# Cluster sums in bf16 parts for half of each third unit, and folded before the selection matmul

## The reference

```python
idx = jnp.argmax(sim, axis=1)                    # sim: normalised x against normalised centroids
onehot = jax.nn.one_hot(idx, N, dtype=x.dtype)
sum_x = jnp.einsum('bhwn,bchw->bnc', onehot, x)  # the cluster sums
count = jnp.sum(onehot, axis=(1, 2))
centroids_local = sum_x / jnp.maximum(count, 1.0)[..., None]
gathered = centroids_local[jnp.arange(B)[:, None, None], idx]
delta = jnp.transpose(gathered, (0, 3, 1, 2)) - x
alpha = jnp.exp(-jnp.mean(delta * delta, axis=1, keepdims=True))
y = x + alpha * delta
out = relu(jnp.einsum('oc,bchw->bohw', W, y) + b)
```

## Time and profile before

| | us |
|---|---|
| median of three runs | 411.43 (411.01 to 411.76) |
| the profiled execution | 411.51 |
| its span in the trace | 409.7 |
| outside the span | 1.8 |
| TensorE busy | 404.5 (99%) |
| VectorE busy | 334.1 (82%) |
| GpSimd busy | 262.9 (64%) |
| ScalarE busy | 257.6 (63%) |

### The profile page before, as it was taken

How to read it: one execution, slowest core, us unless ns; L and a number is a source line. 1 busy time by engine, 2 the same in 40 slices (tenths; PEclk the granted TensorE clock), 3 DMA queues, 4 the chain that set the end, 5 groups by cost and what they waited for, 6 DMA issues and landing times.

```text
span 409.7 us, 5780 instructions
## 1 busy us (share of the span) xinstructions
PE 404.5 (99%) x2090; PEld 289.8 (71%) x2095; DVE 334.1 (82%) x408; ACT 257.6 (63%) x355; POOL 262.9 (64%) x117
## 2 busy tenths in 40 slices
PE   9999999999999999999999999999999999999997
PEld 6755476775777677775867757776777758777886
DVE  3349999788989879899798889898798996898730
ACT  6666774677565594665764676655846657576641
POOL 2003874975699486993789846995869937434420
PEclk9999999999999999999999999999999999999999
DMA  8993574969598596957879485984956240222213
GB/s 268 373 239 55 107 241 93 300 222 218 175 268 201 138 267 148 274 157 191 240 205 269 143 205 172 257 229 133 263 147 215 105 141 2 102 102 104 102 71 136
DMA packets 77917, 74.51 MB, mean 182 GB/s; under 512 B 13722, under 2 KB 52890, under 8 KB 77890
## 3 DMA queue, kind: packets, MB, share of 16 engines
q1 hardware_dynamic: 77890, 74.15, 65.1%
HBM read 46.22 MB, written 25.17 MB: 174 GB/s over the span
## 4 chain that ended last, share of the span: by engine, by line
PE 96%; POOL 1%; ACT 1%; issue 0%; DVE 0%; ACTq 0%; POOLq 0%
PE main L983 21%; PE main L984 21%; PE main L985 21%; PE fa L878 11%; PE sump L923 8%; PE gat L961 5%; PE fa L887 1%; PE al L967 1%; PE main L1043 1%; PE al L1021 1%; PE main L996 1%; PE al L972 1%; POOL o L379 1%; POOL o L382 1%; PE gat L996 0%; PE main L1014 0%
## 5 line engine op out<-in xcount | busy, mean ns | idle before, releaser
L983 PE MATMUL main<-yh,wh 128*128 128x512 f32 (+1 forms) x376 | 152.8, 406 | 0.0
L984 PE MATMUL main<-yl,wh 128*128 128x512 f32 (+1 forms) x376 | 146.3, 389 | 0.0
L985 PE MATMUL main<-yh,wl 128*128 128x512 f32 (+1 forms) x376 | 146.2, 389 | 0.0
L357 POOL TENSOR_TENSOR z<-z,x 128x1024 f32<-128x1024 f32 x41 | 98.5, 2421 | 67.8 <-DVE z L504 67.8
L364 POOL TENSOR_TENSOR yl<-z,yh 128x1024 fp32r<-128x1024 f32 x43 | 103.7, 2432 | 8.2 <-ACT yh L669 8.1
L677 ACT ACTIVATE o<-main,bcol 128x512 f32<-128x512 f32 x96 | 65.2, 681 | 58.5 <-PE main L985 58.2
L983 PEld LDWEIGHTS main<-yh,wh 128*128 128x128 f32 x376 | 70.6, 188 | 21.4 <-issue 4.6
L985 PEld LDWEIGHTS main<-yh,wl 128*128 128x128 f32 x376 | 70.6, 188 | 15.0
L984 PEld LDWEIGHTS main<-yl,wh 128*128 128x128 f32 x376 | 70.7, 188 | 13.9
L371 POOL TENSOR_TENSOR xr<-xt 128x2048 f32<-128x2048 f32 x11 | 51.5, 4682 | 18.2 <-DVE xt L408 18.2
L471 DVE TENSOR_TENSOR z<-gat,x 128x1024 f32<-128x1024 f32 x46 | 56.0, 1218 | 5.4 <-PE gat L961 5.1
(11 more groups left out here) (137 smaller groups left out, 398.2 us busy)
## 6 DMA issues: line engine op xcount, KB each, us to landing
out<-o SPq DMA_DIRECT2D x23, 1024.0 KB, 7.2
x<-x SPq DMA_DIRECT2D x21, 1024.0 KB, 6.8
xs<-x SPq DMA_DIRECT2D x76, 256.0 KB, 5.5
x<-x SPq DMA_DIRECT2D x12, 256.0 KB, 4.5
o<-w SPq DMA_DIRECT2D x1, 1024.0 KB, 8.6
out<-o SPq DMA_DIRECT2D x3, 256.0 KB, 2.0
out<-o SPq DMA_DIRECT2D x2, 128.0 KB, 1.7
oht<-oh SPq DMA_TRANSPOSE x7, 3.7
```

The lines of the kernel that those rows point to most:

```text
L357: pool.tensor_tensor(z, z, X[g // PARTS % 2][:, pair(h), span(g)], ALU.add).then_inc(y_pool, 1)
L983: t_.matmul(tile, WH[:, k, rows], YH[g % 2][:, k, cols], start=(k == 0), stop=False)
L984: t_.matmul(tile, WH[:, k, rows], YL[g % 2][:, k, cols], start=False, stop=False)
L985: last = t_.matmul(tile, WL[:, k, rows], YH[g % 2][:, k, cols], start=False, stop=(k == KC - 1))
```

## The change

1. `split(g)` now returns a number of tiles: four for places 0 and 1 as before, two (HALF) for place 2 of images 2 to 7. So the first two tiles of six units (8, 11, 14, 17, 20, 23) are summed in three bf16 parts too. GpSimd makes their first rest into a new buffer `XRH`, VectorE their second rest.
2. The third unit's other two tiles are summed first, in float32, and its split half last. A pair of matmuls now takes neighbouring tiles.
3. From image 1 on the two halves of `sumP` are added before the high part is made: ScalarE moves the upper half to `upper_sum` (`move_sums`), VectorE adds (`fold_clusters`), ScalarE makes the high part (`copy_sums`), VectorE the low part into partitions 64 to 103 of the same tile, and `add_halves` is one matmul. It stands behind nine of the twelve matmuls of the convolution's second block.
4. VectorE's transposes stand three in the first step, one in the second and two in the third. `add_squares` is cut into `add_pair` (twice) and `add_pairs`, with `low_clusters` between the two.

```diff
 def split(g):
-    return g > 2 * PARTS and g % PARTS < SPLIT
+    return (TILES if g % PARTS < SPLIT else HALF) if g > 2 * PARTS else 0
...
 def sum_order(b):
-    return (0, 1, 2) if b == 0 else (1, 2, 0) if b == 1 else (2, 0, 1)
+    order = (0, 1, 2) if b == 0 else (1, 2, 0)
+    if b < 2:
+        return [(u, range(HALF)) for u in order]
+    return [(2, range(1, HALF)), (0, range(HALF)), (1, range(HALF)), (2, range(1))]
...
+        XRH = sb("xrh", [P, HALF, C], F32)
...
             def first_rest(g):
                 pool.wait_ge(tr_done, by_vector(g))
-                xt = XT[:, g % PARTS, :, :]
-                pool.tensor_tensor(XR[:, g % PARTS, :, :].rearrange("p t c -> p (t c)"),
+                xt = XT[:, g % PARTS, 0:split(g), :]
+                pool.tensor_tensor(rests(g % PARTS).rearrange("p t c -> p (t c)"),
...
             def second_rest(g):
                 dve.wait_ge(rest1_done, splits(g))
-                xr = XR[:, g % PARTS, :, :]
+                xr = rests(g % PARTS)
...
+            def fold_clusters(b):
+                dve.wait_ge(moved_done, b)
+                own = sumP[column_tiles[0], :]
+                v_.tensor_tensor(own, upper_sum[0:N, :], own, ALU.add).then_inc(folded_done, 1)
+
             def low_clusters(b):
                 dve.wait_ge(sumsH_done, b + 1)
...
+                    dve.wait_ge(cop_done, b)
+                    v_.tensor_tensor(sumsH[column_tiles[1], :], sumP[column_tiles[0], :],
+                                     sumsH[column_tiles[0], :].bitcast(F32), ALU.subtract).then_inc(sumsL_done, 1)
...
                 if beside and p < 2:
-                    transpose_half(g + 4, 0)
+                    transpose_half(g + 4, p)
+                if beside and p == 2:
+                    fold_clusters(b + 1)
+                    counts(b + 1)
+                add_pair(g, 0)
                 if beside and p == 2:
                     low_clusters(b + 1)
-                    counts(b + 1)
-                add_squares(g)
+                add_pair(g, 1)
+                add_pairs(g)
                 if beside and p == 0:
                     transpose_half(g + 4, 1)
                 fold(g)
+                if beside and p == 0:
+                    transpose_half(g + 5, 0)
...
                     first_best(b + 1)
-                    transpose_half(g + 4, 1)
...
-                if g + 3 < UNITS and split(g + 3):
+                if p < SPLIT and g + 3 < UNITS and split(g + 3):
                     second_rest(g + 3)
+                if p == 1 and g + 4 < UNITS and split(g + 4):
+                    second_rest(g + 4)
...
             def move_upper(g):
                 act.wait_ge(s_done, folded(g))
+                act.wait_ge(folded_done, min((g + 1) // PARTS, BATCH - 1))
...
+            def move_sums(b):
                 act.wait_ge(c_done, PARTS * (b + 1))
-                wait(act, cop_done, b)
-                a_.activation(sumsH[:, :], sumP[:, :], ACT.Copy).then_inc(sumsH_done, 1)
+                wait(act, fold_done, folded(PARTS * b - 2))
+                a_.activation(upper_sum[0:N, :], sumP[column_tiles[1], :], ACT.Copy).then_inc(moved_done, 1)
...
                 square(g, 0)
                 if beside and p == 2:
+                    move_sums(b + 1)
+                    count_onehot(b + 1)
+                    square(g, 1)
                     copy_sums(b + 1)
-                    count_onehot(b + 1)
                     high_half(g - 1, 0)
-                    square(g, 1)
                     relu(g - 2, 0)
...
                     convolve(g - LAG, 0)
+                    convolve(g - LAG, 1, ks=range(KC - 1))
                     add_halves(b + 1)
+                    convolve(g - LAG, 1, ks=range(KC - 1, KC))
```

More of the change, by code:

```diff
@@ L69, in split @@
 def split(g):
-    return g > 2 * PARTS and g % PARTS < SPLIT
+    return (TILES if g % PARTS < SPLIT else HALF) if g > 2 * PARTS else 0
 def splits(g):
-    return sum(split(i) for i in range(g + 1))
+    return sum(split(i) > 0 for i in range(g + 1))
 def sum_order(b):
-    return (0, 1, 2) if b == 0 else (1, 2, 0) if b == 1 else (2, 0, 1)
+    order = (0, 1, 2) if b == 0 else (1, 2, 0)
+    if b < 2:
+        return [(u, range(HALF)) for u in order]
+    return [(2, range(1, HALF)), (0, range(HALF)), (1, range(HALF)), (2, range(1))]
 def by_vector(g):
@@ L569, in _ @@
             y_half(0, 1)
+            fold_clusters(1)
+            scale(1, 0)
             low_clusters(1)
-            scale(1, 0)
             scale(1, 1)
@@ L780, in _ @@
             high_half(0, 0)
-            copy_sums(1)
+            move_sums(1)
             exp(1)
             high_half(0, 1)
+            copy_sums(1)
             count_onehot(1)
@@ L911, in sum_clusters @@
                     pe.wait_ge(xe_act, 2 * u + 1)
[L912 to L920, removed]
-                        for h in range(2):
[L922 to L927, removed]
+                for t in pairs:
+                    tiles = XT[:, u, HALF * t:HALF * (t + 1), :]
+                    x_parts, onehot = (tiles.rearrange("p t c -> p (t c)"),), oh[:, :, :]
+                    if HALF * t < split(PARTS * b + u):
+                        pe.wait_ge(oh3_done, b + 1)
+                        pe.wait_ge(rest2_done, splits(PARTS * b + u))
+                        left = rests(u)[:, HALF * t:HALF * (t + 1), :]
+                        x_parts = (halfword(tiles, 1), halfword(left, 1), halfword(left, 0))
+                        onehot = oh3[:, :, 0:NPAD]
+                    for j, x_part in enumerate(x_parts):
+                        for h in range(2):
+                            last = t_.matmul(sumP[NPAD * h:NPAD * (h + 1), :], onehot[:, slot(u, HALF * t + h), :],
+                                             x_part[:, h * C:(h + 1) * C],
+                                             start=(opens and t == pairs[0] and j == 0),
+                                             stop=(closes and t == pairs[-1] and j == len(x_parts) - 1))
+                if closes or b < 2 or u < SPLIT:
+                    last.then_inc(c_done, 1)
             def add_halves(b):
@@ L932, in add_halves @@
                 rows = select[:, :]
-                t_.matmul(mean(b), rows, sumsH[:, :], start=True, stop=False)
-                t_.matmul(mean(b), rows, sumsL[:, :], start=False, stop=True).then_inc(cop_done, 1)
+                last = t_.matmul(mean(b), rows, sumsH[:, :], start=True, stop=(b > 0))
+                if b == 0:
+                    last = t_.matmul(mean(b), rows, sumsL[:, :], start=False, stop=True)
+                last.then_inc(cop_done, 1)
             def gather(g, h):
@@ L973, in sum_squares_direct, with convolve @@
                           ).then_inc(one_done, 1)
-            def convolve(g, o, cols=slice(0, UNIT)):
-                wait(pe, relu_done, KC * g + o - 1)
+            def convolve(g, o, cols=slice(0, UNIT), ks=range(KC)):
+                if ks[0] == 0:
+                    wait(pe, relu_done, KC * g + o - 1)
                 rows = slice(o * P, (o + 1) * P)
                 tile = main[:, o % 2, cols] if cols.start == 0 else second_half
-                for k in range(KC):
+                for k in ks:
                     if o == 0 and k % 2 == 0:
@@ L1080, in _ @@
             gather(1, 1)
-            sum_clusters(1, 1)
-            sum_clusters(1, 2)
-            sum_clusters(1, 0)
+            for i in range(PARTS):
+                sum_clusters(1, i)
             gather(2, 0)
@@ L1122, in _ @@
                         similarities(3 * b + 5)
-                convolve(g - LAG, 1)
+                    convolve(g - LAG, 1)
                 if beside and p == 1:
```

38 lines of the change are left out of this document (27 added, 11 removed).

## The result

The changed kernel takes 421.1 us (median of four runs, 420.92 to 422.25) against 411.6 for the kernel before: a ratio of 1.0227, with a 95% interval of 1.0212 to 1.0241. It is slower by 9.5 us; the forecast was 9.3 us, to 420.8. The profiled execution has a span of 419.1 us against 409.7.

What follows compares the result with a forecast made beforehand. TensorE (47.89 us a window) and a VectorE, ScalarE and GpSimd loop (about 47.75) both bound the kernel. The loop's 10.2 us less 0.9 gives 9.3 on 411.5: 420.8 us, range 414.5 to 424 (chance 0.80).

Steps and rivals of the forecast that it cites:

- Two bounds on top of each other: Steady windows: the VectorE, ScalarE and GpSimd loop takes about 47.75 us, just under TensorE's 47.89.
- The port: End of second step: VectorE waits 1.5 us for GpSimd's half first rest; the third step's first delta starts 1.6 us later.
- First step, nothing: First step: the third transpose (1.16 us) fits the 1.34 us idle time ahead of `low_sum`, so it costs nothing.
- Third step, `fold` 1.8 us late: Third step: ScalarE's longer queue delays `move_upper`, so `fold` starts at 201.85 in place of 200.05, +1.8 us.
- The sum: Six windows: +1.2 us in the first, +1.8 in five, 10.2 in all; less 0.9 at the tail, 9.3 us.
- half of the port wait hidden: Case within the forecast's range: 0.75 us a window hidden, six times 0.7 us less, giving 416 us.
- TensorE's saving: TensorE alone gains 2.7 us (1.1 from half units' sums, 1.6 from selection matmuls), which turns into its idle time.
- TensorE stays the bound: Rival: the loop has more than 0.14 us of slack, so TensorE's gain shows, 408.8 us; chance 0.09.
- The port wait is hidden: Rival: half first rest runs in GpSimd's idle time, window 0.15 us longer, 412.3 us; chance 0.06.
- late block loads: Rival: first-step transposes wait 1 us a window more for their block's load, 425 us or more; chance 0.05.

Runs made afterwards that it cites:

- i: The kernel before with 3 of the 12 matmuls of each convolution block left out: 404.3 us, window 47.83 us.
- e: The changed kernel without GpSimd's six half first rests, VectorE's half second rests kept: 413.6 us, window 48.33 us.
- f: The changed kernel without VectorE's six half second rests (8 columns in their place), GpSimd's half first rests kept: 414.5 us, window 48.56 us.
- g: The changed kernel with the transposes where they stood before the change, two in each step: 430.9 us, window 51.24 us.
- j: The changed kernel, but GpSimd's half first rest waits by semaphore until unit 1's second rest is done: 426.6 us, window 50.45 us.
- c: The kernel before with only the new transpose places and the third unit's new tile order, no half rests, no fold: 412.1 us, window 47.91 us.
- b: The changed kernel without the fold: cluster sums copied, split and selected as before, half rests and new transposes kept: 420.3 us, window 49.40 us.
- a: The changed kernel without the half rests; fold, one selection matmul and new transpose places kept: 410.0 us, window 47.67 us.
- k: The changed kernel with 3 of the 12 matmuls of each convolution block left out: 415.7 us, window 49.72 us.

## Why the prediction was right

- *Two bounds on top of each other.* Confirmed by i: without 8.2 us of TensorE's work the window is 47.83 us. I had read 47.75 out of ScalarE's relu that started 0.14 us late; the slack is 0.05. The chain of i has no TensorE in it, so the loop is there. But much of it runs over GpSimd's low halves and first rests, which my list of the loop left out.
- *The port.* The second rest of unit 1 takes 4.08 us where I had 1.5 of waiting and 2.45; the half first rest 1.89 (1.80), the half second rest 1.26 (1.25). e puts the wait at 1.43 us a window and f the work at 1.20. One sentence of this step was off: that the sum stays if VectorE goes first. It loses the head start, 0.37 us in g; j, which forces that order by a semaphore, costs 0.7 us a window more.
- *First step, nothing.* Confirmed by the traces: 2.00 and 2.01 us from `fold` to `low_sum`. c could not have shown it, since TensorE holds its window. g puts the cover at 1.11 us a window (1.16 forecast), without the turn at the port.
- *Third step, `fold` 1.8 us late.* It is 1.87, with the idle time of 1.50 that I had worked out. b gives the fold with its longer ScalarE queue a share of 0.36 us in the window, where I had 0.2 (1.8 less 1.6).
- *The sum.* `fold` in the third step of the six windows is late by 1.06, 2.56, 4.43, 6.29, 8.19 and 10.06 us. I had 1.2 for the first and 1.8 for each of the others, 10.2 in all; the second added only 1.5, the later ones 1.87. The changed kernel's second window is no shorter than its others (49.76 us); the kernel before took 48.26 in that one, with a wait of VectorE for a gather. The first `fold` (g = 3) came 0.36 us earlier than before, so the first window itself added 1.42. The first gather of the tail starts at 358.05 in place of 348.64, 9.4 us late (9.3 forecast), so 0.65 us are lost from the loop to TensorE where I had 0.9, and the tail adds nothing. That the total is right to 0.2 us is in part luck: these deviations of 0.2 to 0.4 us cancel. The mechanism does not rest on it. Taken off or put back one at a time, the runs give 47.83 for the loop before, 1.43 for the wait, 1.20 for the work, 0.36 for the fold and 1.11 back for the transpose: 49.71, and 49.76 was measured. Two small slips in the working change nothing: half of the port wait hidden gives 416.3 to 416.6 and not 416, and the ScalarE distances that I listed end at 201.3, not 201.2.
- *TensorE's saving.* The matmul is there: 0.24 us a window between c and a. The 0.18 us of the half unit can't be read, as TensorE stands in the middle of the sums, and no run isolates them.
- *The rivals.* "TensorE stays the bound" is refuted by i and k. "The port wait is hidden" would have been a window 0.15 us longer; e, which is that kernel without the wait, has 48.33, 0.45 longer, and 413.6 us, so even this case would have been a loss. Of late block loads there is no trace: VectorE waits for no DMA in the windows.

The version that comes out of it, a, takes 410.0 us and beats both. One thing was left untested: GpSimd's whole first rest in the first step stands 2.4 us at the port (5.96 us at 223.42 against 3.60 us at 210.43) and lies on the chain, in the kernel before with less TensorE work (i) as well.

## What to carry to other kernels

An engine that is 99% busy can share the bound with a loop of the others, and the page's chain may name only one of the two: here TensorE with 96% before, although the loop was 0.05 us a window behind it. Before moving work to "idle" engines, look for what their idle times wait for, and take away some of the first engine's work: if the length of the window stays, the other engines are the bound. Where two instructions on VectorE and GpSimd take turns, as the rests here, the engine that waits pays for both, and its wait stands in the profile as a longer instruction (4.08 in place of 2.6 us), not as idle time. So place the pair where one of the two engines waits anyway; in the changed kernel GpSimd stands 6 us behind its half first rest (190.9 to 196.96). Whether the half rests would be free there was not tried.

## What the runs showed of the hardware

In no trace did a second rest on VectorE (two inputs and the output in SBUF) run beside an instruction of GpSimd with two SBUF inputs for more than 0.1 us: it took 2.6 us alone, and 4.1 when due 0.3 us behind a 1.89 us instruction. The low part, with one input in PSUM, took 0.69 us at 25.69 in the kernel before, where GpSimd stood, and 0.68 at 200.96 in the changed one, beside GpSimd; `fold_clusters`, also with one input in PSUM, took 0.67 to 0.75 us, always beside GpSimd. This is what the Trainium skill says ("SBUF — State Buffer", section "SBUF: two separate sides"): the lock concerns a VectorE instruction with two SBUF inputs against a GpSimd instruction that reads SBUF. Unexpected was the price of an order by semaphores in place of the port: 0.14 us from VectorE's end to GpSimd's start in j, and 4.71 us for the pair of rests where the port alone, with VectorE first too, took 4.33 (g).
